# Edge stages of a graph-attention and mixture-of-experts kernel: one-hots from spread 16-bit codes in place of transposes, and four gather buffers in place of three

## The chip, the cores and the metric

The kernel runs on one core of one Trainium2 chip. The metric is the device time of one execution in microseconds. The core has five engines that run their own instruction streams and wait for each other on semaphores: PE (matrix products, with PEld for its weight loads), DVE (vector), ACT (activation functions, copies), POOL (here: indirect DMAs) and SP (here: plain DMAs).

## The reference, cut to what matters

6,250 nodes with 256 features; 100,000 edges, sorted by their target node `dst`. The part that the change touches is a two-layer graph attention network with four heads of 64 features:

```python
def gat_conv(x, src, dst, W, a_src, a_dst, b):
    h = (x @ W).reshape(-1, H, C)
    alpha_s = jnp.einsum('nhc,hc->nh', h, a_src)
    alpha_d = jnp.einsum('nhc,hc->nh', h, a_dst)
    e = jax.nn.leaky_relu(alpha_s[src] + alpha_d[dst], NEG_SLOPE)
    m = jax.ops.segment_max(e, dst, num_segments=N)
    ex = jnp.exp(e - m[dst])
    s = jax.ops.segment_sum(ex, dst, num_segments=N)
    alpha = ex / (s[dst] + 1e-16)
    out = jax.ops.segment_sum(h[src] * alpha[:, :, None], dst, num_segments=N)
    return out.reshape(-1, H * C) + b
...
    x0 = jax.nn.relu(gat_conv(x, src, dst, W1, att_src1, att_dst1, b1))
    x2 = gat_conv(x0, src, dst, W2, att_src2, att_dst2, b2)
```

Beside it stand a linear attention over all nodes (keys and values normalised per head, `dots = k^T v`, then `q @ dots`), whose result is added to the graph network's and to x, and a mixture of 16 experts (two per node) with a layer norm at the end.

## The kernel before

**Stages.** `prepare_edges` turns the sorted `dst` into codes; `project_inputs` makes the table of projected features in DRAM (6,250 rows of 256 features and 4 attention terms, `GW` = 260) and stores the normalised inputs transposed (`xnT_d`); `gat_edges` runs twice, once per layer, with a short stage of bounds between; then the experts are ordered and computed. This page is about `prepare_edges` and the two calls of `gat_edges`.

**Tiling.** The nodes are 49 tiles of 128 (`NT`). The edges are 98 chunks (`NC`) of 1024 (`CE`), each 8 rows of 128 (`KT` = 8). As `dst` is sorted, the edges of a chunk point into a window of at most two neighbouring tiles; a code says which row of the window. One pass over the chunks is enough for these inputs.

**One chunk.** POOL gathers the 1024 rows of the table with eight indirect DMAs (L912) into one of `SLOTS` = 3 buffers `gathered`. DVE writes a one-hot matrix `hot` in bf16 (L948: iota compared with the code, edges on the partitions) and the window's attention terms `dwin` (L597, L598). PE transposes `hot` in eight steps (`turn`, L1196), ACT copies the result to `hotT` (`turned`, L1090) and `hot` to f32, `hotf` (`floats`, L1086). PE takes the targets' terms with `hotT` (`targets`, L1189), DVE makes the logits (`edge_logits`, L957 to L962), ACT the exponentials (`exps`, L1094, L1095), DVE scales the gathered rows in place (`edge_scale`, L968), PE sums them into window rows with `hotf` (`add`, 16 matmuls, L1204), and DVE adds these to the accumulator `acc` (`gain`, L976). `add` counts the semaphore `added`; the gathers of chunk c wait for that of chunk c-3:

```python
def gather(g, c, q, par, use):
    pool.wait_ge(s[f"idx_in{q}"], 16 * use + 16)
    hold(pool, s["added"], g + 1, s["tick"])
    for k in range(KT):
        pool.indirect_dma_start(...)
```

**Tile work between.** Every second step of an engine also does the work of one node tile: in layer 0 the attention's keys and values (PE L1212, L1218; DVE L1000, L1009; ACT L1112, L1118), its dots (L1226), and dividing, turning (L1234) and projecting (L1240) the finished nodes; in layer 1 the mix (L1263 to L1266) and the gates (L1279).

**Order.** The order is written out by hand. `skewed` runs steps of a list (offset, step): at step t of an engine, a step of offset o treats chunk t-o, in the order of the list. So DVE's list `(1, edge_logits), (-1, one_hot), (6, keys), (1, edge_scale), (3, gain), (5, denominators), (5, sums)` takes the logits of chunk t-1, the one-hot of chunk t+1, and so on. PE's list in layer 0 is `(1, targets), (8, project), (0, turn), (7, fin_turn), (7, dots), (2, add), (3, values), (4, keys)`. Engines run in order, so one that waits holds up all that follows on it. SP loads the index lists (`load`, L870), which wait for the logits of the chunk three back, and the tile's inputs (`load_x`, L880), which wait in layer 0 for `keys` and `values` of the tile three back.

Of the kernel before, what the change touches and what calls it, by code (L numbers as in the profile page):

```python
# [15 lines left out]
F32 = mybir.dt.float32  # L16
BF16 = mybir.dt.bfloat16
I32 = mybir.dt.int32
U32 = mybir.dt.uint32
# [15 lines left out]
SLOTS = 3  # L35
# [99 lines left out]
def build(nc, a, out):  # L135
# [5 lines left out]

    srcp = scratch("srcp", (NC * CE,), I32)
    xnT_d = scratch("xnT_d", (NT, P, C))
# [6 lines left out]
    with ExitStack() as top:  # L150
# [27 lines left out]
        with ExitStack() as gnn:  # L178
# [7 lines left out]
            vs = [w1[:, 11 + b, 0] for b in range(SLOTS)]  # L186
            xnT = [w1[:, 4 + b, 0, 0:C] for b in range(SLOTS)]
# [4 lines left out]
            code = sb("code", [P, NC * KT], F32, gnn)  # L192
            code_r = sb("code_r", [P, NC * KT], F32, gnn)
# [10 lines left out]
            edges = (identb, iota, acc, own, peak, parts, windows)  # L204
            stage(prepare_edges, a, srcp, ident, identb, ones, iota, eps, code, lower, upper, first_tile, passes)
# [20 lines left out]
def prepare_edges(nc, a, srcp, ident, identb, ones, iota, eps, code, lower, upper, first_tile, passes, sem):  # L226
# [4 lines left out]
    with ExitStack() as ctx:  # L231
# [5 lines left out]
        partition = sb("partition", [P, 1])  # L237
# [6 lines left out]
        high = sb("high", [NC, CE])  # L244
        ends = sb("ends", [P, 2])
# [13 lines left out]
        s = {n: sem("e_" + n) for n in ("filled", "loaded", "stored", "consts", "steps", "turned", "rowed", "spread", "tiled", "zeroed")}  # L259
# [5 lines left out]
        def _(sp):  # L265
# [7 lines left out]
            sp.wait_ge(s["stored"], 32)  # L273
# [13 lines left out]
        def _(dve):  # L287
# [16 lines left out]
            dve.tensor_reduce(ends[0:NC, 1:2], high[:], AX.X, ALU.max).then_inc(s["tiled"], 1)  # L304
            chain.link(dve.tensor_scalar(dst_i[:], dst_i[:], P - 1, None, ALU.bitwise_and))
# [440 lines left out]
def gat_edges(nc, layer, srcp, table, identb, iota, acc, own, peak, parts, windows, attention, last, sem):  # L746
# [5 lines left out]
    with ExitStack() as ctx:  # L752
# [8 lines left out]
        dwin = sb("dwin", [P, SLOTS, 6 * H], BF16)  # L761
        half = sb("half", [P, SLOTS, 6 * H], BF16)
        G = sb("gathered", [P, SLOTS, KT, GW])
        hot = sb("hot", [P, SLOTS, KT, P], BF16)
        hotf = sb("hotf", [P, SLOTS, KT, P])
        hotT = sb("hotT", [P, SLOTS, KT, P], BF16)
# [7 lines left out]
        psT = pb("psT", [P, KT, P], BF16)  # L774
        psA = pb("psA_e", [P, 2, 512])
        if attention:
# [4 lines left out]
            psDW = pb("psDW_e", [P, 512])  # L781
# [46 lines left out]
        def chunks(eng, begin, end, *stages):  # L828
# [3 lines left out]
            with eng.Fori(0, rounds) as r:  # L832
                def told(step):
                    return lambda c, k, u: step(r * NC + c, c, k % SLOTS, k % 2, r * len(range(k % SLOTS, NC, SLOTS)) + u * 2 + k // SLOTS)
# [917 lines left out]
```

## Time and profile before

| | us |
|---|---|
| three runs | 3338.29, 3321.86, 3336.28 |
| their median | 3336.28 |
| the profiled execution | 3329.73 |
| its span in the trace | 3328.1 |
| layer 0's edge stage, start to end | 200 to 1426 |
| layer 1's edge stage, start to end | 1487 to 2700 |

The rows further down come from the one profiled execution. Times are in us unless marked ns. "Busy" is the time in which an engine has an instruction under way; the time in brackets behind an instruction is what its engine sat idle ahead of it, with what the profile takes to have released it ("issue": nothing that the profile shows; "remote": a semaphore without a known sender). Where an instruction waits for several semaphores, the one named can be another than the one that came last.

### The profile page before, as it was taken

What the parts mean: (1) busy time and instruction counts of PE and PEld (TensorE: products, weight loads), DVE (VectorE), ACT (ScalarE), POOL (GpSimd) and SP (SyncE); (2) the same over time, 40 slices, a digit from 0 to 9 for tenths busy, and PEclk for the clock granted to TensorE, in tenths of its full rate; (3) what the DMA queues carried; (4) which work ended last, traced back from release to release, by engine and by line L of the source; (5) the groups of instructions that cost most, each with busy time, mean ns of one, the idle gap of its engine ahead of it and who ended that gap; (6) DMA issues with size and microseconds to landing.
All of it is one profiled execution on the core that took longest, in us unless ns stands there. A gap on an engine that the chain in (4) does not pass through costs nothing. (4 is left out here: it accounts for less than half of the span.)

```text
span 3328.1 us, 53733 instructions
## 1 busy us (share of the span) xinstructions
PE 2231.7 (67%) x11831; PEld 1712.6 (51%) x11832; DVE 1730.3 (52%) x4175; ACT 1302.8 (39%) x2646; POOL 1946.3 (58%) x1918
## 2 busy tenths in 40 slices
PE   0726667677667667744665666666666755999996
PEld 0424455455445455433454544444544545999984
DVE  3645455555555555564554554454554556555545
ACT  0514344444444444431333433333433333444445
POOL 0256666666566666627666666666666631666654
PEclk9968788888888888877777777777777777999998
DMA  2623333333333333333344433333343325556545
GB/s 52 210 77 93 98 98 95 94 100 94 94 100 95 93 96 95 97 111 101 104 112 107 111 107 104 106 105 106 102 112 107 106 74 149 104 103 105 103 93 167
DMA packets 245595, 347.83 MB, mean 105 GB/s; under 512 B 87442, under 2 KB 184105, under 8 KB 245513
## 3 DMA queue, kind: packets, MB, share of 16 engines
q0 software_dynamic: 101728, 251.76, 30.5%
q1 hardware_dynamic: 103081, 52.72, 6.3%
q10 hardware_dynamic: 40720, 42.61, 3.8%
q8 instruction: 24, 0.39, 0.0%
q14 instruction: 42, 0.34, 0.0%
HBM read 292.90 MB, written 54.42 MB: 104 GB/s over the span
## 5 line engine op out<-in xcount | busy, mean ns | idle before, releaser
L912 POOL DMA_INDIRECT gathered<-table,idx x1568 | 1594.3, 1017 | 859.4 <-issue 452.5
L1204 PE MATMUL psA_e<-gathered,hotf 128*128 128x260 f32 x3136 | 873.6, 433 | 112.7 <-issue 87.3
L1204 PEld LDWEIGHTS psA_e<-gathered,hotf 128*128 128x128 f32 x3136 | 668.2, 219 | 259.5 <-issue 117.9
L1090 ACT ACTIVATE hotT<-psT 128x1024 bf16<-128x1024 bf16 x196 | 199.6, 1019 | 890.3 <-DMA x_in<-in_x 815.6
L968 DVE TENSOR_TENSOR gathered<-gathered,psDW_e 128x2048 f32<-128x2048 f32 x98 | 224.0, 2286 | 315.8 <-ACT psDW_e L1095 269.0
L968 DVE TENSOR_TENSOR gathered<-gathered,psW_e 128x2048 f32<-128x2048 f32 x98 | 223.9, 2285 | 244.8 <-ACT psW_e L1095 205.4
L1086 ACT ACTIVATE hotf<-hot 128x1024 f32<-128x1024 bf16 x196 | 206.1, 1052 | 273.7 <-remote 129.8
L1615 POOL DMA_INDIRECT moe_d<-xscaled,xtarget x113 | 179.3, 1587 | 124.6 <-DVE xtarget L1559 53.8
L948 DVE TENSOR_TENSOR hot<-iota,code_r 128x1024 bf16<-128x1024 bf16 x196 | 240.1, 1225 | 2.9 <-issue 2.9
L1587 PEld LDWEIGHTS xpsH<-xxT,w1e 128*128 128x128 f32 x1808 | 220.7, 193 | 6.2 <-ACT xxT L1516 0.4
L1596 PE MATMUL xpsO<-w,hidT 128*128 x904 | 217.1, 383 | 9.4 <-DVE hidT L1548 8.0
L1587 PE MATMUL xpsH<-xxT,w1e 128*128 128x128 f32 x1808 | 221.4, 276 | 0.0
L1196 PE MATMUL psT<-identb,hot 128*128 128x128 bf16 x1568 | 153.4, 256 | 66.5 <-DVE hot L948 62.5
L1189 PE MATMUL psD_e<-dwin,hotT 128*128 128x24 bf16 x784 | 35.8, 177 | 224.0 <-ACT hotT L1090 199.5
L1596 PEld LDWEIGHTS xpsO<-w,hidT 128*128 128x128 f32 x904 | 163.4, 191 | 31.7 <-issue 13.4
L1548 DVE TENSOR_SCALAR hidT<-xpsH,b1T 128x128 f32<-128x128 f32 x452 | 127.3, 344 | 92.8 <-issue 45.8
L1196 PEld LDWEIGHTS psT<-identb,hot 128*128 128x128 bf16 x1568 | 129.6, 119 | 88.5 <-DVE hot L948 62.8
L1189 PEld LDWEIGHTS psDW_e<-dwin,hotT 128*128 128x128 bf16 x784 | 33.0, 101 | 270.0 <-issue 268.6
L1212 PE MATMUL psKV<-w 128*128 128x512 f32 x196 | 115.1, 717 | 75.2 <-ACT w L1114 57.4
L1218 PE MATMUL psKV<-w 128*128 128x512 f32 x196 | 113.7, 709 | 74.7 <-issue 40.0
L1189 PE MATMUL psDW_e<-dwin,hotT 128*128 128x24 bf16 x784 | 36.0, 177 | 189.2 <-issue 137.0
L1189 PEld LDWEIGHTS psD_e<-dwin,hotT 128*128 128x128 bf16 x784 | 31.3, 99 | 255.5 <-ACT hotT L1090 218.2
(309 smaller groups left out, 3415.9 us busy)
## 6 DMA issues: line engine op xcount, KB each, us to landing
gathered<-table,idx POOLq DMA_INDIRECT x1568
w<-in_L_ffn_w ACTq DMA_DIRECT2D x8, 2048.0 KB
xb<-in_L_ffn_b SPq DMA_DIRECT2D x113, 128.0 KB
w<-xnT_d SPq DMA_DIRECT2D x98, 128.0 KB
table<-acc POOLq DMA_DIRECT2D x49, 130.0 KB, 2.5
table<-acc ACTq DMA_DIRECT2D x49, 130.0 KB
xnT_d<-xnT ACTq DMA_DIRECT2D x49, 128.0 KB, 1.8
xf_d<-w ACTq DMA_DIRECT2D x49, 128.0 KB
```

The costliest lines, as they stand in the source:

```text
L912: pool.indirect_dma_start(out=G[:, q, k, :], out_offset=None, in_=table, in_offset=bass.IndirectOffsetOnAxis(ap=idx[:, q, k:k + 1], axis=0 ...
L948: dve.tensor_tensor(hot[:, q, :, :], iota[:].rearrange("p (k f) -> p k f", k=1).to_broadcast([P, KT, P]), code_r[:, ds(c * KT, KT)].rearra ...
L968: dve.tensor_tensor(f, f, w, ALU.mult).then_inc(s["scaled"], 1)
L1086: act.activation(hotf[:, q, :, :], hot[:, q, :, :], ACT.Copy).then_inc(s["hotf"], 1)
L1090: act.activation(hotT[:, q, :, :], psT[:], ACT.Copy).then_inc(s["hotT"], 1)
L1189: ins = pe.matmul(psD[:, 2 * k:2 * k + 2, :, :].rearrange("p g c h -> p (g c h)"), hotT[:, q, k, :], dwin[:, q, :], start=True, stop=True)
L1196: ins = pe.transpose(psT[:, k, :], hot[:, q, k, :], identb[:])
L1204: ins = pe.matmul(psA[:, par, 0:GW], hotf[:, q, k, :], G[:, q, k, :], start=(k == 0), stop=(k == KT - 1))
L1548: dve.tensor_scalar(hidT[:, q % 2, k * P:(k + 1) * P], psH[:, q % 2, k * P:(k + 1) * P], b1T[:, ds(e, 1), k:k + 1].rearrange("p o k -> p ( ...
L1587: ins = pe.matmul(psH[:, q % 2, k * P:(k + 1) * P], w1e[:, q % 2, kc, k * P:(k + 1) * P], xT[:, q % 2, kc, :], start=(kc == 0), stop=(kc = ...
L1596: ins = pe.matmul(psO[:, q % 2, 0:C], hidT[:, q % 2, k * P:(k + 1) * P], w2[:, ds(e, 1), k, :].rearrange("p o f -> p (o f)"), start=(k == ...
L1615: pool.indirect_dma_start(out=moe_d, out_offset=bass.IndirectOffsetOnAxis(ap=target[:, q % 2:q % 2 + 1], axis=0), in_=scaled[:, q % 2, :], ...
```

## The change

1. `prepare_edges` also computes the code of every edge in chunk order, 98 x 1024, as 16-bit integers, permuted so that the edges of row k lie together, and stores it in DRAM (`codes_d`).
2. Per chunk, SP loads the 1024 codes of the chunk to all 128 partitions (a broadcast of 2 KB to each, `load_codes`, one chunk ahead). DVE compares them with the partition's number (`mark`) and so writes `hotT` at once. PE's `turn` and ACT's `turned` and `floats` are gone.
3. A new DVE step `placed`, behind `edge_scale`, writes `hotf` in f32; it waits for the sums of two chunks back. `hotf`, `hotT`, `dwin` and `half` have two buffers.
4. `SLOTS` is 4: four buffers of `gathered` and `idx`; the loop is unrolled over 4 chunks and no longer over 6. The tile buffers (`x`, `xnT`, `vs`) are `TURN` = 2, and the counts of the tile semaphores follow.
5. In layer 0 the targets' terms and the weights have PSUM banks of their own, and `targets` no longer waits for the last scaling. PE's list of steps is otherwise as it was.

```diff
-SLOTS = 3
+SLOTS = 4
+TURN = 2
...
+            chain.link(dve.tensor_scalar(rel_c[:], low[:], ends[0:NC, 0:1], None, ALU.subtract))
+            dve.tensor_scalar(residue_c[:], by_chunk_i[:], P - 1, None, ALU.bitwise_and)
+            chain.link(dve.tensor_scalar(rel_c[:], rel_c[:], 7, None, ALU.arith_shift_right))
+            dve.wait_ge(s["tiled"], 1)
+            dve.tensor_copy(high[:], residue_c[:])
+            chain.link(dve.tensor_copy(low[:], rel_c[:]))
+            chain.link(dve.scalar_tensor_tensor(low[:], low[:], float(P), high[:], ALU.mult, ALU.add))
+            dve.tensor_scalar(code_c[:].rearrange("c (k p) -> c p k", k=KT), low[:].rearrange("c (p k) -> c p k", k=KT), float(1 << 14), None, ALU.min).then_inc(s["coded"], 1)
...
             def load(g, c, q, par, use):
-                sp.wait_ge(s["logits"], g + 1)
+                hold(sp, s["logits"], g + 1, s["tick"])
...
+            def load_codes(g, c, q, par, use):
+                hold(sp, s["hotT"], g + 1, s["tick"])
+                sp.dma_start(codes[:, par, :], codes_d[ds(c * CE, CE)].rearrange("(o e) -> o e", o=1).to_broadcast([P, CE])).then_inc(s[f"codes_in{par}"], 16)
...
-                rounds = chunks(sp, new_pass(sp), nothing, (0, load), (1, load_x, True))
+                rounds = chunks(sp, new_pass(sp), nothing, (0, load), (-1, load_codes), (1, load_x, True))
...
             def one_hot(g, c, q, par, use):
-                dve.tensor_tensor(hot[:, q, :, :], iota[:].rearrange("p (k f) -> p k f", k=1).to_broadcast([P, KT, P]),
-                                  code_r[:, ds(c * KT, KT)].rearrange("p (k f) -> p k f", f=1).to_broadcast([P, KT, P]), ALU.is_equal).then_inc(s["hot"], 1)
+
+                dve.wait_ge(s[f"codes_in{par}"], g * 8 - par * 8 + 16)
+                dve.tensor_scalar(hotT[:, par, :, :].rearrange("p k f -> p (k f)"), codes[:, par, :], mark[:, 0:1], None, ALU.is_equal).then_inc(s["hotT"], 1)
...
+            def placed(g, c, q, par, use):
+                dve.wait_ge(s["added"], g + SLOTS - 1)
+                dve.tensor_tensor(hotf[:, par, :, :], iota[:].rearrange("p (k f) -> p k f", k=1).to_broadcast([P, KT, P]),
+                                  code_r[:, ds(c * KT, KT)].rearrange("p (k f) -> p k f", f=1).to_broadcast([P, KT, P]), ALU.is_equal).then_inc(s["hotf"], 1)
...
-                rounds = chunks(dve, both_new(dve), next_pass, (1, edge_logits), (-1, one_hot), (6, keys, True), (1, edge_scale), (3, gain), (5, denominators, True), (5, sums, True))
+                rounds = chunks(dve, both_new(dve), next_pass, (1, edge_logits), (-1, one_hot), (6, keys, True), (1, edge_scale), (0, placed), (3, gain), (5, denominators, True), (5, sums, True))
...
-            def floats(g, c, q, par, use):
-                act.wait_ge(s["hot"], g + 1)
-                act.wait_ge(s["added"], g + 1)
-                act.activation(hotf[:, q, :, :], hot[:, q, :, :], ACT.Copy).then_inc(s["hotf"], 1)
-
-            def turned(g, c, q, par, use):
-                act.wait_ge(s["turned"], g + 1)
-                act.activation(hotT[:, q, :, :], psT[:], ACT.Copy).then_inc(s["hotT"], 1)
...
             def targets(g, c, q, par, use):
                 pe.wait_ge(s["dwin"], g + 1)
-                pe.wait_ge(s["hotT"], g + 2)
+                pe.wait_ge(s["hotT"], g + 3)
                 pe.wait_ge(s["target_read"], g + 1)
-                if attention and later(c, 1):
-                    pe.wait_ge(s["scaled"], g)
...
-            def turn(g, c, q, par, use):
-                pe.wait_ge(s["hot"], g + 1)
-                pe.wait_ge(s["hotT"], g + 1)
-                for k in range(KT):
-                    ins = pe.transpose(psT[:, k, :], hot[:, q, k, :], identb[:])
-                ins.then_inc(s["turned"], 1)
...
-                chunks(pe, nothing, nothing, (1, targets), (8, project, True), (0, turn), (7, fin_turn, True), (7, dots, True), (2, add), (3, values, True), (4, keys, True))
+                chunks(pe, nothing, nothing, (1, targets), (8, project, True), (7, fin_turn, True), (7, dots, True), (2, add), (3, values, True), (4, keys, True))
```

## Rows read from the trace of the kernel before

**Rows 1.** The profile's page, busy time of the engines and one DMA queue over the span.
```profile
PE 2231.7 (67%) x11831; PEld 1712.6 (51%) x11832; DVE 1730.3 (52%) x4175; ACT 1302.8 (39%) x2646; POOL 1946.3 (58%) x1918
...
q1 hardware_dynamic: 103081, 52.72, 6.3%
```

**Rows 2.** Table of stretches, the two edge stages: length, busy us (instructions) of each engine, PE's clock, DMA share, GB/s.
```profile
200.00:1426.00 1226.00, 827.28 (x4108) 586.46 (x4109) 648.20 (x1202) 511.29 (x988) 794.19 (x784) 0.82 0.36 96
...
1487.00:2700.00 1213.00, 766.21 (x3845) 574.18 (x3846) 603.66 (x1249) 436.77 (x844) 799.33 (x784) 0.75 0.40 110
```

**Rows 3.** Groups of instructions by line and form: busy us, mean ns, idle time before, its releasers.
```profile
L912 POOL DMA_INDIRECT gathered<-table,idx x1568 | 1594.3, 1017 | 859.4 <-issue 452.5 <-remote 239.6 <-PE psA_e L1204 156.3
L1204 PE MATMUL psA_e<-gathered,hotf 128*128 128x260 f32 x3136 | 873.6, 433 | 112.7 <-issue 87.3 <-DVE acc L976 21.1 <-DVE dwin L598 2.4
...
L948 DVE TENSOR_TENSOR hot<-iota,code_r 128x1024 bf16<-128x1024 bf16 x196 | 240.1, 1225 | 2.9 <-issue 2.9
L968 DVE TENSOR_TENSOR gathered<-gathered,psDW_e 128x2048 f32<-128x2048 f32 x98 | 224.0, 2286 | 315.8 <-ACT psDW_e L1095 269.0 <-issue 42.5 <-ACT gathered L1094 4.2
...
L1086 ACT ACTIVATE hotf<-hot 128x1024 f32<-128x1024 bf16 x196 | 206.1, 1052 | 273.7 <-remote 129.8 <-issue 112.6 <-DVE hot L948 22.1
L1090 ACT ACTIVATE hotT<-psT 128x1024 bf16<-128x1024 bf16 x196 | 199.6, 1019 | 890.3 <-DMA x_in<-in_x 815.6 <-issue 43.4 <-PE psT L1196 31.1
...
L1196 PE MATMUL psT<-identb,hot 128*128 128x128 bf16 x1568 | 153.4, 256 | 66.5 <-DVE hot L948 62.5 <-issue 4.0
```

**Rows 4.** The gathers of one stage, layer 0 above, layer 1 below: ns min/median/max; idle us, times.
```profile
L912 POOL DMA_INDIRECT gathered<-table,idx x784: 942/949/3035, 200.2 to 1425.0; - x196
...
  remote: 114.1, 44
  PE psA_e L1204: 93.9, 35
...
  remote: 125.6, 47
  PE psA_e L1204: 62.4, 21
```

**Rows 5.** Timeline of layer 0, 1107 to 1114 us: start, length, engine, line, idle time before.
```profile
1107.79 0.61 PE L1196 MATMUL psT<-identb,hot 128*128 128x128 bf16 x8
...
1108.24 3.73 PE L1204 MATMUL psA_e<-gathered,hotf 128*128 128x260 f32 x16
...
1112.94 1.02 ACT L1090 ACTIVATE hotT<-psT 128x1024 bf16<-128x1024 bf16 x1 [4.57 <-DMA x_in<-in_x]
```

**Rows 6.** Timeline of layer 0, 983 to 1002 us.
```profile
984.85 0.61 PE L1196 MATMUL psT<-identb,hot 128*128 128x128 bf16 x8
...
991.50 0.20 DVE L960 TENSOR_TENSOR z_e<-both_e,gathered 128x32 f32<-128x32 f32 x1 [0.16 <-DVE both_e L957]
...
996.96 0.94 POOL L912 DMA_INDIRECT gathered<-table,idx  x1 [0.31 <-issue]
1000.32 1.02 ACT L1090 ACTIVATE hotT<-psT 128x1024 bf16<-128x1024 bf16 x1 [16.08 <-DMA x_in<-in_x]
...
1001.39 0.95 POOL L912 DMA_INDIRECT gathered<-table,idx  x1 [3.49 <-remote]
```

**Rows 7.** Timeline at the start of layer 0, 234 to 253 us.
```profile
235.47 6.26 PE L1204 MATMUL psA_e<-gathered,hotf 128*128 128x260 f32 x16
...
251.97 1.02 ACT L1090 ACTIVATE hotT<-psT 128x1024 bf16<-128x1024 bf16 x1 [14.48 <-DMA x_in<-in_x]
```

**Rows 8.** Timeline of layer 0, 906 to 910 us.
```profile
908.06 1.23 DVE L948 TENSOR_TENSOR hot<-iota,code_r 128x1024 bf16<-128x1024 bf16 x1
...
908.32 1.78 POOL L912 DMA_INDIRECT gathered<-table,idx  x1 [0.30 <-issue]
```

**Rows 9.** Timeline of the first preparation stage, 28 to 46 us.
```profile
30.10 0.69 DVE L301 TENSOR_SCALAR high<-low 98x1024 f32<-98x1024 f32 x1
```

**Rows 10.** The profile's page, DMA issues: KB each, us from issue to landing.
```profile
table<-acc POOLq DMA_DIRECT2D x49, 130.0 KB, 2.5
```

More of the change, by code:

```diff
@@ L18 @@
 I32 = mybir.dt.int32
+I16 = mybir.dt.int16
 U32 = mybir.dt.uint32
@@ L203, in build @@
             windows = (code, code_r, lower, upper, first_tile, window_tile, passes)
-            edges = (identb, iota, acc, own, peak, parts, windows)
-            stage(prepare_edges, a, srcp, ident, identb, ones, iota, eps, code, lower, upper, first_tile, passes)
+            edges = (codes_d, partition, iota, acc, own, peak, parts, windows)
+            stage(prepare_edges, a, srcp, codes_d, partition, ident, identb, ones, iota, eps, code, lower, upper, first_tile, passes)
             spare = w1[:, 14:16].rearrange("p e k f -> p (e k f)")
@@ L743, in _, with gat_edges @@
                 passes_over(pe, lambda r: None, step)
-def gat_edges(nc, layer, srcp, table, identb, iota, acc, own, peak, parts, windows, attention, last, sem):
+def gat_edges(nc, layer, srcp, table, codes_d, partition, iota, acc, own, peak, parts, windows, attention, last, sem):
     with ExitStack() as ctx:
@@ L760, in gat_edges @@
         code, code_r, lower, upper, first_tile, window_tile, passes = windows
-        dwin = sb("dwin", [P, SLOTS, 6 * H], BF16)
-        half = sb("half", [P, SLOTS, 6 * H], BF16)
+        dwin = sb("dwin", [P, 2, 6 * H], BF16)
+        half = sb("half", [P, 2, 6 * H], BF16)
         G = sb("gathered", [P, SLOTS, KT, GW])
-        hot = sb("hot", [P, SLOTS, KT, P], BF16)
-        hotf = sb("hotf", [P, SLOTS, KT, P])
-        hotT = sb("hotT", [P, SLOTS, KT, P], BF16)
+        codes = sb("codes", [P, 2, CE], I16)
+        mark = sb("mark", [P, 1])
+        hotf = sb("hotf", [P, 2, KT, P])
+        hotT = sb("hotT", [P, 2, KT, P], BF16)
         both = sb("both_e", [P, 2 * KT, H])
@@ L813, in gat_edges @@
             one = sb("one", [P, NT])
-        names = ["idx_in0", "idx_in1", "idx_in2", "g_in0", "g_in1", "g_in2", "hot", "turned", "hotT", "hotf", "targets", "dwin", "own", "own_weights",
+        names = ["idx_in0", "idx_in1", "idx_in2", "idx_in3", "g_in0", "g_in1", "g_in2", "g_in3", "codes_in0", "codes_in1", "hotT", "hotf", "targets", "dwin", "own", "own_weights",
                  "own_terms", "target_read", "logits", "weights", "scaled", "added", "acc", "pass", "dests", "dest_steps", "vsteps", "logit_steps", "tick",
@@ L896, in load_x @@
                     sp.dma_start(xnT[b], xnT_d[ds(i, 1), :, :].rearrange("o p f -> (o p) f")).then_inc(s[f"x_in{b}"], 16)
-                rounds = chunks(sp, new_pass(sp), nothing, (0, load), (6, load_x, True))
+                rounds = chunks(sp, new_pass(sp), nothing, (0, load), (-1, load_codes), (6, load_x, True))
             hold(sp, s["stored"], rounds * (PER_STORE * NT) + PER_STORE, s["tick"])
@@ L1141, in _ @@
                 act.wait_ge(s["constants"], 32)
-                chunks(act, new_dest(act), nothing, (9, store, True), (6, roots, True), (0, floats), (0, turned), (1, exps), (6, divide, True), (5, squares, True), (7, relu, True), (8, copies, True))
+                chunks(act, new_dest(act), nothing, (9, store, True), (6, roots, True), (1, exps), (6, divide, True), (5, squares, True), (7, relu, True), (8, copies, True))
             else:
```

81 lines of the change are left out of this document (43 added, 38 removed).

## The prediction

> **What bounds the kernel now.** I read the busy shares first: no engine is full over the span, PE stands at 67%, POOL at 58%, DVE at 52%, ACT at 39% [rows 1]. The change touches only the first preparation stage and the two edge stages, so the next view is the table by stage. Its two long windows, 200 to 1426 and 1487 to 2700 us, are the edge stages, each with 784 gathers (98 chunks of 8), at 794 and 799 us of POOL, and with PE, DVE and ACT below that or near it [rows 2]. The period is 1226 / 98 = 12.51 us per chunk in layer 0 and 1213 / 98 = 12.38 in layer 1.
>
> A gather takes 1017 ns in the mean [rows 3], and the waits of POOL say what lies between: most gaps are 0.30 us and put down to issue. A train of eight gathers therefore costs 8 x (1.017 + 0.305) = 10.6 us (from the windows (794.19 + 784 x 0.305) / 98 = 10.54, and 10.60). The rest, 12.45 - 10.57 = 1.88 us per chunk, is a pause: POOL waits for `added`, that is until PE has summed the chunk three back and so given its buffer free. 44 + 35 of layer 0's 98 pauses carry such a releaser, 208 us together, and 47 + 21 of layer 1's, 188 us [rows 4]. So POOL's own work sets the period, at 85% of it, and the sums' release of a buffer sets the other 15%. All of the pauses are worth 1.88 x 196 = 368 us, which is the most that any change which leaves the gathers as they are can win here.
>
> Why are sums late? A chunk's way from its landed gather to its sums is short: about 1 us of logits, 2 of exponentials, 2.3 of scaling, 3.7 of matmuls [rows 3, 5], some 10 us against three periods of 37. What stretches it is seen in the timeline. At 1107.79 PE transposes a one-hot in 0.61 us, and ACT's copy of it, idle for 4.57 us, starts only at 1112.94, when the train of gathers has ended [rows 5] (the view names an old DMA as releaser; by the code ACT waits for `turned`). At 984.85 the same transposes end at 985.46, POOL runs on without a break to 997.9, and the copy comes at 1000.32, after 16.08 us [rows 6]; at the start of layer 0, 14.48 us [rows 7]. The signal of a PE group that ends while POOL is deep in unbroken gathers thus seems to be seen only when POOL pauses. ACT is in order, so exponentials, scaling, sums and the release queue up behind it. Over all, ACT idled 890 us ahead of that copy [rows 3].
>
> **The change, part by part.**
>
> *Removed:* per chunk 8 transposes on PE (153.4 / 196 = 0.78 us), the copies L1086 (1.05 us) and L1090 (1.02 us) on ACT [rows 3]. Neither engine is the bound, so by busy time this buys nothing; what it buys is one late signal fewer in the chain of each chunk, and ACT free to take the exponentials as logits come. In layer 0 also the wait of `targets` on the last scaling.
>
> *Fourth buffer:* a gather now needs the sums four back. By itself: up to the 1.88 us per chunk, if sums then never come late.
>
> *Added on DVE per chunk:* `hotT` by one comparison of 1024 16-bit codes with a scalar. No row shows it. Bounds: above, the two-input comparison of the same size, 1.225 us [rows 3]; below, half of the nearest row, a tensor_scalar over 1024 f32 at 0.69 us [rows 9]. I take 0.69. The f32 one-hot (`placed`) is the same two-input form as L948 and replaces it: 1.225 for 1.225. DVE's busy time in layer 0 goes from 648 / 98 = 6.6 to 7.3 us per chunk, with some nine gaps of 0.16 us [rows 6] 8.7 us: under 10.6, so hidden while nothing holds DVE. The page "VectorE: DVE Perf Modes" of the Trainium skill (Mode 4x_2P) gives 16-bit operands in SBUF four elements per cycle, an estimate of 0.42 us here; no row shows it, and either is hidden.
>
> *Contention:* the gather that L948 meets is longer: 1.78 us at 908.32 beside L948 at 908.06 [rows 8]. The mean of all gathers, 1017 against 949 ns of an undisturbed one (as at 996.96, 0.94 us [rows 6], and the median of the gathers [rows 4]), is 0.068 x 1568 = 106 us, 0.54 us per chunk, and it is already inside the 10.57. `placed` keeps it. What `hotT` adds is between nothing (other tensor_scalars show no stretched gather) and in proportion of durations, 0.54 x 0.42 / 1.225 = 0.19 us: 0 to 37 us over 196 chunks. I take 18. The Trainium skill, "SBUF — State Buffer" (the section "SBUF: two separate sides", its box on DVE and SWDGE), says that a DVE instruction in a two-port mode holds the port pair with which GpSimd writes descriptors, and blocks it wholly. That rule speaks against this change, because `hotT` is a form that can enter such a mode; for operations with two SBUF inputs the trace has the stretched gathers above, for the two-port mode it shows nothing. With the page's 0.42 us for `hotT`, blocked in full, the 18 us would be an estimated 82, and the time 64 us later, still in the likeliest case's range.
>
> *Codes:* 196 broadcasts of 256 KB = 51 MB, as much as queue q1 carries now at 6.3% of the DMA engines [rows 1], where the stages show a DMA share of 0.36 and 0.40 [rows 2]. Taken as nothing; the cover is that the load is issued one chunk ahead, some 10 us before DVE needs it. Bounds: 0 to 196 x 0.1.
>
> *SP's order:* with two tile buffers, `load_x` of a tile in layer 0 now waits for the keys of two tiles back, work of the PE step just before, and SP has queued behind it the index list of the next even chunk. If the sums run at pace the list comes in time; if PE is late, POOL waits for a list. Its landing is not shown; the nearest is 2.5 us for a tile's store [rows 10]. Bounds 0 to 49 x 2.5 = 122 us; I take 0.5 us each, 24 us, as PE has no work after the keys and its step starts before POOL's train ends. In layer 1 `load_x` waits on `mixed`, work of much earlier, 0.
>
> *Prologue:* seven DVE operations on [98, 1024]: five one-input ones at 0.69 [rows 9], one two-input at L948's 1.225 [rows 3], and one with a permuted 16-bit output between 0.69 and 1.225: 5.4 to 5.9 us, with gaps 6, on DVE's path of that stage. The store of codes lies under DVE's remaining work.
>
> *The new wait:* `placed` of chunk t stands in DVE's queue behind the scaling of t-1 and waits for the sums of t-2. Before, DVE waited for sums only in `gain`, one step later. Behind it queue gain, denominators, the next logits, `dwin` and `hotT`, then the next scaling; PE's targets wait for those, POOL for the sums. With x from the end of a scaling to its sums seen, two steps take x + 8.7 us, so the period is (x + 8.7) / 2. Sums alone take 3.7 us (6.26 at the lower clock at 235.47 [rows 5, 7]): 6.2 to 7.5 us, no bound. It becomes one against 10.57 from x = 12.4, a signal late by 8.7 us, and makes the kernel slower from x = 16.2, late by 12.5 us.
>
> **How it could go.**
>
> *Likeliest (0.43): late signals stay, and cost one pause in three chunks.* The transposes' signal is gone but `targets` and `added` are signals of PE too, and nothing in the change makes them pass during unbroken gathers. POOL with four buffers runs more trains on end, then pauses as before, and such a pause after two unbroken trains is 3.49 us [rows 6]; I take 3.2, between that and the mean of those with a releaser, 396 / 147 = 2.7 [rows 4]. With one in three chunks: (3 x 10.57 + 3.2) / 3 = 11.63, which saves 0.82 x 196 = 161 us. One in two would be 12.17 (saves 55), one in four 11.37 (saves 212). Sum, against the profiled execution of 3329.7: 3329.7 - 161 + 6 + 18 + 24 = 3217. The median of the runs shown is 6.6 us above that execution, so 3223, given as 3220. Its own range is 3130 to 3330: 3329.7 - 212 + 6 + 6.6 = 3130 with no contention and no list waits, 3329.7 - 55 + 6 + 18 + 24 + 6.6 = 3329 at the other end.
>
> *A (0.25): POOL becomes the whole bound.* If late signals were the transposes' alone, or four buffers cover any lateness, all 368 us go: 3329.7 - 368 + 6 + 18 + 0 to 37 (list or landing waits) + pauses at layer ends of 15 = 3001 to 3038, with the median's 6.6 3008 to 3045; its centre is put at 3040, up to 3090 if a part of the pauses stays. For it: the unhindered way of a chunk is some 10 us against four trains of 42. Against it: lateness grew with the length of the unbroken run (4.57, 14.48, 16.08 us).
>
> *C (0.13): no gain.* The release is tied to POOL's own pause: buffers only shift when it comes, the pause grows from 1.9 to what the signals' backlog needs, and 12.45 per chunk stays: 3329.7 + 6 to + 48, with the median 3342 to 3385 at worst, and 3320 to 3350 for most of it.
>
> *D (0.19): slower, by the new wait in `placed`.* With sums seen 14 us late (between the 14.48 and 16.08 of a run of two or more trains and the 4.57 of one), x = 17.7 and the period is 13.2 us: + 0.75 x 196 = 147, + 6, so 3483, with the median 3490; at 12.5 us late it only breaks even. For it: longer unbroken runs are just what a fourth buffer makes. Against it: POOL has to stop for lack of buffers when DVE stands, and the stop lets the signal through, so 14 us can hardly hold for every chunk.
>
> **Numbers.** A change under 0.5% (17 us) is about what a measurement here can't tell from none. Faster: A and most of the likeliest, 0.67. Same: half of C and the edge of the likeliest, 0.12. Slower: D and the rest of C, 0.21. Range for 8 in 10: 3030, which leaves out the faster part of A (0.08), to 3370, which takes in C and leaves out most of D (0.12).
>
> **What would show it.** In the table by stage POOL's busy time stays near 795 to 800 us per layer (more by up to 18 if `hotT` blocks it) while the window shrinks to about 1140; pauses of POOL ahead of a train fall from about one per chunk to one in three, of 3 to 4 us. ACT's 890 us ahead of L1090 vanish, and DVE's wait ahead of the scaling falls from 269 us [rows 3] in layer 0. If A is right, POOL shows hardly any gap over 0.31 us; if D, DVE shows a wait for PE's sums ahead of the f32 one-hot. A wait of POOL on `idx` would show the SP term. I am wrong if the sums' signals turn out prompt, which gives A, or if what looked like a signal held back by POOL was ACT's or PE's own order, where the removal alone decides.

## The result and the profile after

The changed kernel takes 3413.07 us (median of 4 runs, 3408.03 to 3427.99), the kernel before 3334.06 beside it: a ratio of 1.0242, 95% interval 1.021 to 1.0274. It is slower by 79 us, where 3220 was forecast and 3030 to 3370 given as the range.

Every edited kernel below ran in a set with the kernel before beside it, and the kernel before took 3005 to 3012 us in some sets and 3287 to 3330 in others, alike within a set, on two chips in both ways: where it is slow, PE's signals are late, as in the trace that the prediction was made from (the late condition), and where it is fast they are prompt (the prompt condition). Ratios are always to the kernel before of the same set; where two sets are compared, the text says so.

The page of the profiled execution (3408.63 us, span 3407.0) answers [rows 1]:

```profile
PE 2121.5 (62%) x10263; PEld 1611.7 (47%) x10264; DVE 1854.0 (54%) x4382; ACT 934.7 (27%) x2254; POOL 1913.9 (56%) x1918
...
q1 hardware_dynamic: 131417, 104.31, 11.5%
```

DVE works 124 us more, ACT 368 less, and q1 carries the codes, 51.6 MB more. By stretches (edge stage of layer 0, what lies between, edge stage of layer 1), which answers [rows 2]:

```profile
207.00:1493.00 1286.00, 781.97 (x3306) 534.62 (x3307) 702.18 (x1290) 323.68 (x786) 776.72 (x784) 0.78 0.41 111
1493.00:1572.00 79.00, 38.49 (x151) 28.06 (x151) 45.23 (x86) 19.88 (x47) 2.19 (x5) 0.72 0.19 59
1572.00:2773.00 1201.00, 687.10 (x3017) 513.78 (x3018) 650.31 (x1335) 250.57 (x641) 786.19 (x784) 0.76 0.48 131
```

The columns are those of [rows 2]. Taken from first to last gather, the loss of 78.9 us between the two spans (3407.0 - 3328.1) is +7.6 ahead of layer 0, +59.2 in layer 0 (1284.9 against 1225.7), +18.6 between the layers (79.4 against 60.8), -13.1 in layer 1 (1200.7 against 1213.8), and +6.7 behind. POOL's busy time fell in both layers. So the loss is waiting, and most of it is in layer 0.

The groups of instructions by line and form, which answer [rows 3]:

```profile
L930 POOL DMA_INDIRECT gathered<-table,idx x1568 | 1562.9, 997 | 940.0 <-issue 467.3 <-remote 219.1 <-DMA idx<-srcp 217.5
L1212 PE MATMUL psA_e<-gathered,hotf 128*128 128x260 f32 x3136 | 896.7, 448 | 340.2 <-DVE acc L1002 283.7 <-issue 56.5
...
L994 DVE TENSOR_TENSOR gathered<-gathered,psW_e 128x2048 f32<-128x2048 f32 x196 | 446.8, 2280 | 1.0 <-ACT psW_e L1112 0.8 <-issue 0.2
L987 DVE TENSOR_TENSOR hotf<-iota,code_r 128x1024 f32<-128x1024 bf16 x196 | 239.4, 1222 | 367.8 <-remote 305.8 <-PE psA_e L1212 33.6 <-issue 28.1
...
L970 DVE TENSOR_SCALAR hotT<-codes,mark 128x1024 bf16<-128x1024 int16 x196 | 102.2, 521 | 11.6 <-issue 8.0
...
L978 DVE TENSOR_REDUCE both_e<-psD_e 128x64 f32<-128x192 f32 x196 | 68.8, 351 | 322.5 <-remote 260.7 <-issue 61.6
...
L1111 ACT ACTIVATE gathered<-t_e 128x32 f32<-128x32 f32 x196 | 45.0, 229 | 1135.7 <-DVE t_e L983 737.8 <-issue 397.4
```

The gathers are a little shorter (997 against 1017 ns), but POOL idles 940 us ahead of them in place of 859. DVE, which before hardly waited ahead of its one-hot (2.9 us), now waits 368 us there, and PE waits 284 us for DVE's `gain` (L1002), which stands behind that wait. What POOL waits for is told by its gathers, layer 0 above, layer 1 below, as in [rows 4]:

```profile
L930 POOL DMA_INDIRECT gathered<-table,idx x784: 940/946/3214, 207.8 to 1491.7; - x196
...
  DMA idx<-srcp: 204.8, 33
  remote: 58.4, 13
  PE psA_e L1212: 10.6, 5
...
  remote: 160.7, 48
  PE psA_e L1212: 25.6, 16
  DMA idx<-srcp: 12.7, 3
```

In layer 0 the waits for the sums fell from 208 us to 69, and 205 us of waits for the index list `idx` took their place; there were none before. In layer 1 they are 186 us for the sums, as before, and 13 for lists.

One such place, in the timeline of layer 0 at 798 us:

```profile
798.40 2.28 DVE L994 TENSOR_TENSOR gathered<-gathered,psW_e 128x2048 f32<-128x2048 f32 x1
...
802.67 3.77 PE L1212 MATMUL psA_e<-gathered,hotf 128*128 128x260 f32 x16 [0.16 <-DVE acc L1002]
...
808.75 1.98 PE L1226 MATMUL psKV<-w 128*128 128x512 f32 x4 [2.31 <-issue]
...
815.17 0.37 PE L1234 MATMUL psM<-w 128*128 128x128 f32 x1 [2.55 <-issue]
...
818.06 0.37 PE L1234 MATMUL psM<-w 128*128 128x128 f32 x1 [2.52 <-issue]
...
821.13 1.22 DVE L987 TENSOR_TENSOR hotf<-iota,code_r 128x1024 f32<-128x1024 bf16 x1 [10.24 <-remote]
821.26 0.33 SPq L898 DMA_DIRECT2D w<-xnT_d  x1
821.83 0.33 SPq L884 DMA_DIRECT2D idx<-srcp  x1
...
824.25 0.23 ACT L1111 ACTIVATE gathered<-t_e 128x32 f32<-128x32 f32 x1 [15.26 <-DVE t_e L983]
...
824.68 0.94 POOL L930 DMA_INDIRECT gathered<-table,idx  x1 [6.95 <-DMA idx<-srcp]
```

The scaling ends at 800.68, PE's sums run from 802.67 to 806.44. `placed` (L987) waits for these sums and starts at 821.13: they are seen 14.7 us late. The trace's own record of the increment of `added` stands at 820.99, so the increment itself comes late, and DVE acts on it within 0.14 us. PE is slow itself meanwhile: between single matmuls of its dots (L1234) it idles up to 2.55 us, with nothing that the profile shows as the cause. The keys (L1226) end at 810.73; SP's `load_x` waits for them and is issued at 821.26, and only behind it the index list, at 821.83. POOL, which had run on, stands still for 6.95 us until that list has landed. ACT's exponentials have idled 15.26 us. Here both new waits hang on late signals of PE, and both come free together.

### The profile page after: what moved, and what is told of

Same layout as the page of the kernel before. It is cut to its first block and busy times, and to the rows that moved or that the text cites. A ratio compares the mean times of both kernels' runs of the same rounds, so it can differ in the third digit from the quotient of the medians.

```text
span 3407.0 us, 51550 instructions
## 1 busy us (share of the span) xinstructions
PE 2121.5 (62%) x10263; PEld 1611.7 (47%) x10264; DVE 1854.0 (54%) x4382; ACT 934.7 (27%) x2254; POOL 1913.9 (56%) x1918
## 5 line engine op out<-in xcount | busy, mean ns | idle before, releaser
L994 DVE TENSOR_TENSOR gathered<-gathered,psW_e 128x2048 f32<-128x2048 f32 x196 | 446.8, 2280 | 1.0 <-ACT psW_e L1112 0.8
L987 DVE TENSOR_TENSOR hotf<-iota,code_r 128x1024 f32<-128x1024 bf16 x196 | 239.4, 1222 | 367.8 <-remote 305.8
L1111 ACT ACTIVATE gathered<-t_e 128x32 f32<-128x32 f32 x196 | 45.0, 229 | 1135.7 <-DVE t_e L983 737.8
L978 DVE TENSOR_REDUCE both_e<-psD_e 128x64 f32<-128x192 f32 x196 | 68.8, 351 | 322.5 <-remote 260.7
L1204 PE MATMUL psD_e<-dwin,hotT 128*128 128x24 bf16 x1568 | 79.2, 176 | 261.5 <-issue 135.7
L1204 PEld LDWEIGHTS psD_e<-dwin,hotT 128*128 128x128 bf16 x1568 | 73.5, 100 | 355.5 <-issue 287.7
L1226 PE MATMUL psKV<-w 128*128 128x512 f32 x196 | 127.0, 782 | 121.7 <-DVE w L1036 82.1
L1271 PE MATMUL psY<-mixM,w 128*128 128x256 f32 x196 | 70.5, 493 | 157.5 <-ACT w L1172 113.2
L1614 POOL DMA_INDIRECT xx<-xf_d,xsource x113 | 111.4, 986 | 40.0 <-issue 33.6
L1530 ACT ACTIVATE w1e<-w 128x1024 f32 x113 | 119.5, 1057 | 48.6 <-issue 30.7
L1226 PEld LDWEIGHTS psKV<-w 128*128 128x128 f32 x196 | 39.8, 223 | 172.0 <-DVE w L1036 94.7
```

Source lines behind the costliest of these rows:

```text
L987: dve.tensor_tensor(hotf[:, par, :, :], iota[:].rearrange("p (k f) -> p k f", k=1).to_broadcast([P, KT, P]), code_r[:, ds(c * KT, KT)].rea ...
L994: dve.tensor_tensor(f, f, w, ALU.mult).then_inc(s["scaled"], 1)
L1111: act.activation(G[:, q, :, C:GW], t[:], ACT.Exp).then_inc(s["weights"], 1)
L1204: ins = pe.matmul(psD[:, 2 * k:2 * k + 2, :, :].rearrange("p g c h -> p (g c h)"), hotT[:, par, k, :], dwin[:, par, :], start=True, stop=True)
L1226: ins = pe.matmul(psKV[:, 0, :], xnT[b][:, kc * P:(kc + 1) * P], wkvT[:, kc, 0, :], start=(kc == 0), stop=(kc == 1))
L1530: act.activation(w1e[:, q % 2, :, :].rearrange("p k f -> p (k f)"), w1[:, ds(e, 1), :, :].rearrange("p o k f -> p (o k f)"), ACT.Copy).the ...
```

## The experiments

All edits are of the changed kernel, but for two runs of the kernel before. They stand in the order in which they tell most, by the condition in which they ran.

### In the late condition

**Four buffers alone.** The kernel before with `gathered` and `idx` in four buffers, no other part of the change.

```diff
+DEEP = 4
-        G = sb("gathered", [P, SLOTS, KT, GW])
+        G = sb("gathered", [P, DEEP, KT, GW])
-                act.wait_ge(s["added"], g + 1)
+                act.wait_ge(s["added"], g + 2)
-            pe.sem_inc(s["added"], SLOTS)
+            pe.sem_inc(s["added"], DEEP)
```

> The kernel before with four buffers for the gathered rows and the index lists, and nothing else of the change (transposes, copies on ACT and three tile buffers stay; the loop is unrolled over 12 chunks). Theory L (late signals of PE): if the kernel before is near 3334, longer unbroken runs of gathers make the signals later still, and the time is within 20 us of 3334 or above it; theory P (the fourth buffer is what covers lateness) gives 3200 to 3280. Where the kernel before is near 3006, POOL has no pauses left to save, and it is 3006 within 10 us.

3305.95 us against 3286.98, ratio 1.0056 (1.004 to 1.0073). POOL's waits for the sums, idle us and times over both layers:

```profile
  remote: 239.4, 85
  PE psA_e L1205: 112.4, 42
```

352 us of pauses stand with a buffer more (396 in [rows 4], of another set). A buffer more does not cover the lateness; theory P fell. From the last gather of layer 0 to the first of layer 1 this trace has 80.7 us, against 60.8 in the kernel before of the other set.

**Codes to one partition.** The broadcast becomes a load of 2 KB; the other 127 partitions compare with a constant, so the kernel leaves out the targets' terms.

```diff
-                sp.dma_start(codes[:, par, :], codes_d[ds(c * CE, CE)].rearrange("(o e) -> o e", o=1).to_broadcast([P, CE]))
+                sp.dma_start(codes[0:1, par, :], codes_d[ds(c * CE, CE)].rearrange("(o e) -> o e", o=1))
+            dve.memset(codes[:].rearrange("p a e -> p (a e)"), 1 << 14)
```

> The changed kernel with the 1024 codes of a chunk loaded to one partition in place of 128 (2 KB in place of 256 KB; the other partitions compare with a constant, so hotT is zero there and the outputs lack the targets' terms). It takes away 51 MB of DMA. If the broadcast's traffic costs nothing, the time is that of the changed kernel within 5 us (2979 where the kernel before is near 3006, 3413 where it is near 3334); if the traffic is behind the loss, 20 to 79 us less.

3333.39 us against 3286.98, ratio 1.0134 (1.0108 to 1.016). Without 51 MB of traffic it is still slower than the kernel before. POOL's waits for index lists are fewer than in the changed kernel (104 us in 22 places over both layers, against 217 in 36). Whether the 1.1 points to 1.0242 are the traffic or the difference between two sets isn't told apart: the changed kernel was not in this set, whose kernel before is 47 us faster. So a part of the loss may be the traffic's.

**DVE's new wait taken off.** `placed` one step later, between logits and scaling, in both layers.

```diff
-(1, edge_scale), (0, placed), (3, gain)
+(1, placed), (1, edge_scale), (3, gain)
```

> The f32 one-hot between the logits and the scaling, one step later, once more. Where the kernel before is near 3290 to 3334: theory N (DVE's new wait makes the loss) 1.00 or less; else 1.01 to 1.02. Where it is near 3006: 0.978 as in the first run of it.

3376.32 us against 3326.17, ratio 1.0156 (1.0133 to 1.0178). Of the wait ahead of the one-hot 27 us are left, but the chain of waits of DVE, and under it that of POOL (us in total, times, longest), show where it went:

```profile
DVE both_e L978 <- remote: 527.3, 69, 28.2
```

```profile
POOL gathered L930 <- remote: 193.6, 57, 7.4
POOL gathered L930 <- DMA idx<-srcp: 167.8, 27, 11.8
...
POOL gathered L930 <- PE psA_e L1212: 76.4, 22, 7.4
```

DVE now waits 527 us for the targets' terms, another signal of PE; in the changed kernel it was 261 there and 306 ahead of the one-hot. The lateness moved to another instruction of DVE; 0.9 points were won (1.0242 and 1.0156 are of two sets), against the 2.4 of theory N. POOL still waits 168 us for index lists.

**The list's wait taken off too.** SP loads the index list a step earlier, ahead of `load_x`.

```diff
-(0, load), (-1, load_codes), (1, load_x, True)
+(-1, load), (-1, load_codes), (1, load_x, True)
```

> The f32 one-hot between the logits and the scaling, and the index list a step earlier, once more. Where the kernel before is near 3290 to 3334: if the list's wait is the rest of the loss, POOL's waits for it fall from 168 us to under 20 and the ratio from 1.016 to 0.96 to 1.00; if lateness only moves on to POOL's wait for the sums, 1.01 to 1.02. Where it is near 3006: 0.976.

3295.33 us against 3330.03, ratio 0.9898 (0.9875 to 0.992). The two edge stages by stretches, POOL's waits (idle us, times) and DVE's:

```profile
207.00:1395.00 1188.00, 766.46 (x3307) 528.50 (x3308) 704.71 (x1293) 323.90 (x787) 792.13 (x784) 0.82 0.45 120
1468.00:2656.00 1188.00, 697.96 (x3031) 521.77 (x3032) 667.61 (x1341) 253.24 (x646) 779.09 (x784) 0.76 0.49 133
```

```profile
  remote: 310.3, 96
  PE psA_e L1212: 34.7, 20
  DMA idx<-srcp: 10.4, 1
```

```profile
DVE both_e L978 <- remote: 463.7, 81, 28.1
```

Layer 0 is 1188 us long, 97 less than in the changed kernel's own trace, and 84 less than with `placed` moved alone (1271). The waits for lists are gone but for the first of the stage. The two runs that differ by this edit alone are of two sets, whose kernels before agree within 4 us (3326.17 and 3330.03); the edit turns a loss of 1.6% into a gain of 1.0%. This run still has the broadcasts, so their traffic alone does not make the changed kernel slower than the kernel before.

**Three of the four buffers in use.** As the run before, and the gathers of chunk c wait for the sums of c-3.

```diff
-                hold(pool, s["added"], g + 1, s["tick"])
+                hold(pool, s["added"], g + 2, s["tick"])
```

> The same, with the gathers of chunk c waiting for the sums of c-3, so three of the four buffers in use. Where the kernel before is near 3290 to 3334: if longer unbroken runs make the signals later, it is faster than the run beside it, by 10 to 60 us; if the fourth buffer covers lateness, slower by as much. Where it is near 3006: within 0.3% of the run beside it.

3297.81 us against 3330.03, ratio 0.989 (0.9861 to 0.992), the same as the run beside it. The fourth buffer neither helps nor hurts here.

### In the prompt condition

The expectations of the first four edits here (`placed` later, `load_x` later, both, three back) give times for the late condition. These runs fell in the prompt one, so they do not test theories N, S and R there.

**The kernel before.** 

> The kernel before with a profile, for its gaps of POOL and the lateness of PE's signals where its time is near 3006. Theory L: the copy of the transposes on ACT comes under 1 us after PE's transposes end, the period is 10.6 to 10.8 us per chunk, and no pause is over 1 us. Rival: the gathers themselves are shorter there, with the pauses as before.

3004.36 us, in a set where its median is 3006.76. The page has

```profile
L912 POOL DMA_INDIRECT gathered<-table,idx x1568 | 1636.4, 1044 | 491.5 <-issue 469.6
...
L1090 ACT ACTIVATE hotT<-psT 128x1024 bf16<-128x1024 bf16 x196 | 198.8, 1015 | 289.7 <-PE psT L1196 288.6
```

and the timeline of layer 0

```profile
708.95 0.61 PE L1196 MATMUL psT<-identb,hot 128*128 128x128 bf16 x8
...
709.59 1.02 ACT L1090 ACTIVATE hotT<-psT 128x1024 bf16<-128x1024 bf16 x1 [1.94 <-PE psT L1196]
...
709.83 0.95 POOL L912 DMA_INDIRECT gathered<-table,idx  x1 [0.30 <-issue]
```

The transposes end at 709.56, and ACT's copy starts at 709.59, where ACT idled 16.08 us for it in [rows 6]; its idle time ahead of the copy is 290 us in all, for 890. Yet POOL runs here with next to no pause through whole layers: its idle time fell from 859 to 492 us, which is 0.31 a gather. Unbroken gathers alone don't make signals late. Of the copies for which ACT stood idle as the transposes ended, the median starts 0.04 us after them here (96 copies, none over 0.1), and 4.6 us in the trace of [rows 6] (67 copies, the latest 14.9).

**The changed kernel**, twice. 

> The changed kernel once more, with the kernel before beside it. In the four runs before this the kernel before took 3006 us, not 3334, and POOL had no pauses at all. Theory L (late signals of PE, which come and go with the chip or its state, are what makes the change slower): if the kernel before is near 3334 here, the ratio is 1.02 again; if it is near 3006, the changed kernel is near 2980 to 3010, a ratio of 0.99 to 1.00, and layer 0's edge stage has no pauses of POOL over 0.31 us. Theory K (the change costs some 2.4% wherever it runs): 1.02 in either state.

2979.47 us against 3006.76, ratio 0.9911 (0.988 to 0.9943). Theory K fell: the same program is 2.4% slower in one condition and 0.9% faster in the other. POOL is the whole bound in both kernels:

```profile
L930 POOL DMA_INDIRECT gathered<-table,idx x1568 | 1597.8, 1019 | 494.1 <-issue 479.7
```

A gather takes 1019 ns against 1044: 0.025 x 1568 = 39 us less. In the two profiled executions 10 us more in the preparation and 7 between the layers leave 22; the medians differ by 27. The shorter gathers are those that meet DVE's two-input comparison: the 196 that start while `hot` is written take 1682 ns in the mean, the 219 that start while `hotf` is written 1374, and all others some 950 to 960 in both kernels.

> The changed kernel beside the kernel before once more, as the control for the run beside it: a ratio of 1.02 to 1.03 where the kernel before is near 3290 to 3334, 0.99 where it is near 3006.

2983.87 us against 3004.61, ratio 0.9935 (0.9917 to 0.9954).

**`placed` a step later, behind the scaling**, twice. 

> The f32 one-hot is made one step later, (1, placed) in place of (0, placed), in both edge stages: DVE then waits for sums that PE did a step earlier, with a whole step's slack more. Theory N (the new wait holds up DVE): DVE's 368 us of idle time ahead of the one-hot fall below 60, layer 0's edge stage falls from 1285 us to 1226 or less, and the kernel to 3340 or less against 3413 of the changed kernel. Theory S (SP's order, a load of a tile's input that holds up the index list): POOL's 217 us of waits for the list stay and layer 0 stays near 1270 to 1285. Theory B (a bigger load of DVE or of the DMA engines): both stages stay within 1% of the changed kernel's.

> The f32 one-hot a step later, beside the changed kernel itself. Where the kernel before is near 3334: theory N gives 3340 or less, theory S 3380 to 3413. Where it is near 3006: within 1% of the changed kernel, since DVE's wait is then covered.

2982.65 us against 3005.65, ratio 0.9926 (0.9909 to 0.9943), and 2982.66 against 3006.76, 0.9923 (0.9903 to 0.9944): no difference to the changed kernel, as no signal is late.

**`load_x` a step later**, `(2, load_x)`, twice. 

> In layer 0 SP's load of a tile's input stands one step later, (2, load_x) in place of (1, load_x), so that no index list is queued behind a wait for keys of the PE step just before. Theory S: POOL's 217 us of waits for the index list fall below 20, and the kernel by 60 to 140 us, to 3275 to 3350. Theory N: POOL's waits are renamed (for the sums in place of the list), their total of layer 0 stays near 280 us, and the time within 20 us of 3413. Layer 1 is unchanged in both.

> The tile's input loaded a step later, beside the changed kernel itself. Where the kernel before is near 3334: theory S gives 3275 to 3350 and no waits of POOL for the index list in layer 0; theory N gives within 20 us of 3413. Where it is near 3006: within 1% of the changed kernel.

3006.75 us, ratio 1.0008 (0.9996 to 1.0019), and 3006.72, 1.0001 (0.9988 to 1.0015). It costs 27 us against the changed kernel, in layer 0 alone, with longer gathers and no waits. There the gathers that start while `hotf` is written take 1677 ns (100 of them) against 1484 (98), which is 20 us; why they meet it so was not tried. The one wait for a list that is left is that of the start:

```profile
POOL gathered L930 <- DMA idx<-srcp: 12.0, 1, 12.0
```

**Both of these edits**, twice. 

> Both of the edits before together. If N and S are each other's cover (PE late makes the list late, the list late makes PE late), only this one gains in full: 3200 to 3260, with layer 0 near 1140 to 1170 and layer 1 near 1150. If lateness of PE's signals in unbroken gathers is still the bound, as the prediction's likeliest case has it, about 11.6 us per chunk: 3220. If POOL were all of the bound, 10.6 us per chunk: 3040.

> The f32 one-hot and the load of the tile's input both a step later. Where the kernel before is near 3290 to 3334: if the two new waits (DVE for the sums of two chunks back, the index list behind keys of the step just before) make the loss, the ratio falls from 1.02 to 0.96 to 0.99, DVE's wait ahead of the one-hot from some 370 us to under 100, and POOL's for the list from some 220 us to under 20. If late signals bound it in whatever place they are waited for, it stays at 1.00 or above. Where it is near 3006: 1.000, as before.

3006.86 us, ratio 1.0 (0.999 to 1.001), and 3004.98, 1.0002 (0.9991 to 1.0012).

**The gathers of the changed kernel wait for the sums three back.** 

> The changed kernel with the gathers of chunk c waiting for the sums of c-3 (four buffers in memory, three in use), so that POOL runs fewer trains on end. Theory R (the longer unbroken runs make PE's signals late, and that holds up DVE): the waits of DVE ahead of the one-hot shrink from 368 to under 200 us and layer 0 returns to 1230 to 1250 us. Against it: a buffer less can only cost, layer 0 is longer than 1285 us and the kernel slower than 3413.

2985.63 us, ratio 0.9919 (0.989 to 0.9947): where signals are prompt, three buffers are enough.

**`placed` between logits and scaling, the list a step earlier, and both.** 

> The f32 one-hot is made one step later, between the logits and the scaling, (1, placed), (1, edge_scale). Where the kernel before is near 3290 to 3334: theory N (DVE's new wait) gives a ratio of 1.00 or less and DVE's wait ahead of the one-hot under 100 us (366 in the changed kernel); theory S (the index list) leaves 1.01 to 1.02. Where it is near 3006: 0.99, as the changed kernel, or lower by up to 10 us, since the one-hot lies where DVE waits for the exponentials.

2947.36 us against 3012.31, ratio 0.9783 (0.9767 to 0.9799). The gathers are shorter again:

```profile
L930 POOL DMA_INDIRECT gathered<-table,idx x1568 | 1551.0, 989 | 494.5 <-issue 479.8
```

989 ns against 1019: 0.030 x 1568 = 47 us. The one-hot is as long as before (1224 ns), but the gathers that start while it is written, 196 of them, take 1196 ns in the mean and no longer 1374 (219 of them). That makes some 45 of the 47 us. At which point of a gather the one-hot must fall to stretch it less was not tried. The expectation had at most 10 us here.

> SP loads the index list a step earlier, (-1, load), ahead of the wait for keys. Where the kernel before is near 3290 to 3334: theory S gives POOL's waits for the list under 20 us (217 in the changed kernel) and a ratio of 0.99 to 1.00; theory N the same time as the changed kernel, 1.02, with POOL's waits for the sums in place of those for the list. Where it is near 3006: 0.99.

2989.01 us, ratio 0.9918 (0.99 to 0.9936), as the changed kernel.

> Both edits. Where the kernel before is near 3290 to 3334: if the two waits make the loss, 0.96 to 0.99, below either alone; if late signals cost the same wherever they are waited for, 1.00 to 1.01, as with four buffers alone (1.006). Where it is near 3006: 0.99.

2941.84 us, ratio 0.9756 (0.9738 to 0.9774). With both edits the kernel beats the kernel before in both conditions: by 2.4% here and, in the run above, by 1.0%.

## Why the prediction was wrong

**The failing step is the pricing of the two new waits**, that for the sums in `placed` ("no bound" in the likeliest case, its loss left to rival D with 0.19) and that of the index list behind `load_x` (24 us of the sum). With both taken off, the ratio falls from 1.0242 to 0.9898, some 115 us of the 193 by which the forecast missed. **The rest is the term of 161 us for the fourth buffer**, for pauses that the buffer did not take away. Both signs that the prediction named for the waits came: DVE waits 306 us for sums ahead of the one-hot, and POOL 217 us on `idx`. Point by point:

*What bounds it.* The rows were read rightly: POOL at 85% of the period, the late release of buffers at 15%. That signals of PE are late was right for that trace; "when POOL is deep in unbroken gathers" is a necessary part at most, since the prompt condition has unbroken gathers and no lateness.

*The removed work.* As forecast, the 890 us ahead of L1090 are gone, and the wait ahead of the scaling is gone too. But ACT now idles 1136 us ahead of its exponentials (L1111), for DVE: one late signal fewer in the chain, and one more place that waits for another. What the removal is worth by itself was not run. The nearest is the kernel with both waits off and three buffers in use, 1.1% faster than the kernel before.

*The fourth buffer.* Forecast at 161 us, as one pause in three chunks. With both waits off, 310 + 35 + 10 = 355 us of pauses in 117 places stand over 196 chunks, one of 3.0 us in 1.7 chunks, where 396 us were in [rows 4] (another set). The two edge stages are 65 us shorter than in the trace of before, 41 of it pauses and 23 shorter gathers. And even that isn't the buffer's: alone it costs 0.56%, and with three of four in use the time is the same.

*The list.* Priced at 24 us of bounds 0 to 122. Moving it away won 84 us of layer 0 (1271 to 1188, of two sets). The reason given for the low value, that PE has no work after the keys and its step starts before POOL's train ends, took the keys' signal as prompt, while the same text argued that PE's signals are late. The prediction did not ask what the lateness does to SP. Layer 1, where `load_x` waits for old work, shows 13 us of it: forecast at 0.

*The wait in `placed`.* Rival D had the mechanism, but that its number fits is chance: 14 us late for every chunk gives 13.2 us per chunk, and layer 0 has 1284.9 / 98 = 13.1. In fact DVE waits over 0.5 us there for only half of layer 0's chunks, and the sums' lateness in these is anything from 0 to 24 us (median 12). Over all chunks of the layer x is 16.0 us in the mean and not 17.7, and what was put at 8.7 us, from the one-hot to the end of the next scaling, is 10.6, as DVE waits there for the targets' terms as well. D's 13.2 for both layers is wrong for layer 1, which has 12.3 and no loss. With the wait taken off, layer 0 falls only to 1271, since DVE then waits for `targets`. The argument against D, that POOL's own stop lets the signals through, did not keep layer 0 from its loss. Not run in the late condition was the list's edit alone, so whether the wait in `placed` costs anything without the list's is open.

*DVE's new work.* `hotT` was taken at 0.69 us; it takes 521 ns in the mean and 486 in the median. The f32 one-hot takes 1222 ns for 1225. Neither is on the path in the prompt condition. The 0.42 us estimated from the Trainium skill's page "VectorE: DVE Perf Modes" (Mode 4x_2P) is nearer to the 486 ns than the 0.69.

*Contention.* 18 us of loss were taken; it is a gain. Gathers went from 1017 to 997 ns, 1044 to 1019 in the prompt condition. In the changed kernel's prompt trace the 150 gathers that start while `hotT` is written take 1034 ns in the mean, 85 more than 949, 13 us in all. By the Trainium skill's page "SBUF — State Buffer" ("SBUF: two separate sides", the box on DVE and SWDGE) a two-port DVE operation blocks GpSimd wholly, which was estimated at up to 82 us in total; the trace doesn't bear out a full block.

*The codes' traffic.* Taken as nothing. The run without it is 1.34% slower than its kernel before, against 2.42% for the changed kernel in another set; what lies between is not told apart.

*The prologue.* Forecast 6 us, measured 7.6:

```profile
33.96 0.74 DVE L313 TENSOR_SCALAR rel_c<-low,ends 98x1024 int32<-98x1024 f32 x1
...
37.40 1.22 DVE L319 SCALAR_TENSOR_TENSOR low<-low,high 98x1024 f32<-98x1024 f32 x1
38.66 2.45 DVE L320 TENSOR_SCALAR code_c<-low 98x1024 int16<-98x1024 f32 x1
```

The cut stands for four more operations of 0.69 us. The one with the permuted 16-bit output takes 2.45 us, twice the upper bound taken for it; 0.74 + 4 x 0.69 + 1.22 + 2.45 = 7.2, and gaps.

*Not in the sum at all:* the 18.6 us between the layers. A large part seems to come with the fourth buffer: alone it has 80.7 us there, as the changed kernel has 79.4, and with both waits off it is 73.5 with four buffers in use and 69.7 with three (60.8 in the kernel before; three sets). That POOL is further ahead when its last gather ends, and the work behind it is drained at the late signals' pace, fits this but is argued; in the prompt condition it is 64.6 against 57.7. The 6.7 us behind layer 1 stay open.

## What to carry to other kernels

Price a new wait by how late the signal has been seen in this trace, on every queue that takes it, and not by when the work ends; and list what each queue has behind it, the small loads on SP first. A buffer more won nothing here while the same late signals released it. Measure a change in each condition that the kernel before shows: the same program was 2.4% slower in one and 0.9% faster in the other.

## What the runs showed of the hardware that was not expected

The same program of the kernel before takes 3005 to 3012 us in some sets of runs and 3287 to 3334 in others, steadily within a set, on two chips in both ways.

In the slower ones semaphore increments of PE come up to 14 to 16 us after the matmuls' end, and in single cases later (24 us at most ahead of `placed`), while POOL issues indirect DMAs. In the changed kernel's prompt trace the record of every increment of `added` stands within 0.1 us of the last matmul's end. Since the ends of matmuls are modelled, it isn't told whether PE finishes late or its increment travels late.

The lateness is not that of all signals. In the late trace of the changed kernel ACT's exponentials start 0.03 us after DVE's terms (median of 131 that waited; one took 2.0, no other over 1), as in the prompt one (0.03, 153 of them).

PE also idles up to 2.55 us between single matmuls in the late condition. The eight records of L1234 stretch from 811 to 821 us in the changed kernel; in its first run in the prompt condition they take 1.06 us together:

```profile
711.90 1.06 PE L1234 MATMUL psM<-w 128*128 128x128 f32 x8
```

POOL's and DVE's own instructions keep their lengths (the median gather is 946 ns in both of the changed kernel's traces, the f32 one-hot 1222 and 1226 ns). The mean granted clock of TensorE is lower in the late condition (0.82 against 0.86 for the kernel before), but a matmul of the sums is only 4% longer with it (433 against 416 ns), which is no 14 us; whether the clock is a cause or follows from PE's longer idle times isn't shown. What brings the condition about stays open; the same program shows both.

A two-input comparison of DVE (1.22 us) lengthens the indirect DMA that starts beside it: 1682 ns in the mean for 196 of them in the kernel before (prompt condition), against some 950 for the others.
